# Router logits from unnormalised rows, one Perceiver layer on one NeuronCore

## The reference

```python
x = x + xattn(_layernorm(x), ctx_1024, w1_w, w1_b, w2_w, w2_b)
x = x + attn(_layernorm(x), q_w, q_b, k_w, k_b, v_w, v_b, o_w, o_b)
x = x + ffn(_layernorm(x), gate_w, wg, wu, wd)
```

```python
logits = x_flat @ gate_w.T
top_v, top_i = jax.lax.top_k(logits, K)
probs = jax.nn.softmax(top_v)
...
hidden = jax.nn.silu(x_flat @ wge.T) * (x_flat @ wue.T)
acc + we[:, None] * (hidden @ wde.T)
```

## Time and profile before

| | |
|---|---|
| median of 3 runs | 630.2 us (629.74 to 630.58) |
| profiled execution, time | 631.73 us |
| its span, first to last instruction | 629.8 us |
| PE busy | 605.1 us (96%) |
| PEld busy | 517.9 us (82%) |
| DVE busy | 458.3 us (73%) |
| ACT busy | 336.7 us (53%) |
| POOL busy | 262.6 us (42%) |
| mean granted TensorE clock | 0.985 |
| DMA over the span | 244 GB/s |

### The profile page before, as it was taken

The page is one execution under the profiler, slowest core; times in us unless marked ns, Lnnn a source line. Parts: engine busy times, 40 slices in busy tenths (PEclk is TensorE's granted clock), DMA queues, the critical chain, the costliest instruction groups (busy, mean ns, idle before and its releaser), DMA issues.

```text
span 629.8 us, 10827 instructions
## 1 busy us (share of the span) xinstructions
PE 605.1 (96%) x4033; PEld 517.9 (82%) x4033; DVE 458.3 (73%) x812; ACT 336.7 (53%) x603; POOL 262.6 (42%) x318
## 2 busy tenths in 40 slices
PE   8999999899999999998999898999999999999995
PEld 7889988898889988996667676888888888888884
DVE  4877688767977698768888957876767676776851
ACT  4547523672257423563776671665665657565550
POOL 4317920684157532694544542034241423334222
PEclk9999999999999999999999986999999999999999
DMA  8978887899869746862000355899999999999952
GB/s 286 333 301 232 270 316 202 225 281 289 296 195 290 214 115 175 242 173 67 2 2 2 135 215 210 319 328 347 330 339 348 311 357 320 362 330 347 337 186 83
DMA packets 66131, 152.89 MB, mean 243 GB/s; under 512 B 7632, under 2 KB 47952, under 8 KB 55184
## 3 DMA queue, kind: packets, MB, share of 16 engines
q1 hardware_dynamic: 61712, 146.04, 69.4%
q0 software_dynamic: 4368, 6.16, 4.6%
HBM read 121.91 MB, written 31.59 MB: 244 GB/s over the span
## 4 chain that ended last, share of the span: by engine, by line
PE 72%; DVE 9%; POOL 7%; DMA 4%; ACT 4%; issue 3%; POOLq 0%; DVEq 0%; ACTq 0%; SPq 0%
PE psum L1687 17%; PE psum L1297 13%; PE psum L1422 13%; PE psum L1704 10%; PE psum L1462 9%; POOL wide_low L592 4%; PE psum L1372 2%; DMA region_a<-turned_up 2%; DVE head_max L961 2%; DVE region_a L966 1%; POOL wide_high L590 1%; PE psum L1338 1%; PE psum L1302 1%; ACT wide_high L679 1%; PE psum L1505 1%
## 5 line engine op out<-in xcount | busy, mean ns | idle before, releaser
L679 ACT ACTIVATE wide_high<-region_a 128x1024 fp32r<-128x1024 f32 (+1 forms) x108 | 106.6, 997 | 99.7 <-PE psum L1687 92.6
L1127 DVE TENSOR_TENSOR wide_low<-region_a,wide_high 128x1024 fp32r<-128x1024 f32 x92 | 112.2, 1222 | 63.8 <-ACT wide_high L679 63.8
L592 POOL TENSOR_TENSOR wide_low<-region_a,wide_high 128x512 fp32r<-128x512 f32 x64 | 82.5, 1291 | 18.3 <-ACT wide_high L679 14.3
L1704 PE MATMUL psum<-region_a,region_w 128*128 128x256 f32 x368 | 83.4, 379 | 0.5 <-ACT region_w L679 0.5
L1462 PE MATMUL psum<-turned_high,wide_low 128*128 128x256 f32 x256 | 79.6, 311 | 2.4 <-DVE turned_low L1038 1.5
L1687 PE MATMUL psum<-wide_low,turned_high 128*128 128x512 f32 x184 | 79.2, 431 | 0.1
L1704 PEld LDWEIGHTS psum<-region_a,region_w 128*128 128x128 f32 x368 | 69.6, 190 | 11.0 <-issue 0.9
L1687 PE MATMUL psum<-wide_high,turned_low 128*128 128x512 f32 x184 | 73.0, 397 | 0.0
L1687 PE MATMUL psum<-wide_high,turned_high 128*128 128x512 f32 x184 | 72.7, 395 | 0.0
L1462 PE MATMUL psum<-turned_high,wide_high 128*128 128x256 f32 x256 | 72.4, 283 | 0.0
L1462 PE MATMUL psum<-turned_low,wide_high 128*128 128x256 f32 x256 | 72.2, 282 | 0.0
(11 more groups left out here) (221 smaller groups left out, 1225.3 us busy)
## 6 DMA issues: line engine op xcount, KB each, us to landing
region_a<-turned_up SPq DMA_DIRECT2D x23, 2048.0 KB, 9.7
region_a<-turned_down SPq DMA_DIRECT2D x23, 1024.0 KB, 6.8
region_a<-ctx_dram SPq DMA_DIRECT2D x16, 1024.0 KB, 9.0
turned_up<-region_w SPq DMA_DIRECT2D x64, 256.0 KB, 4.2
region_w<-L_ffn_wg_dram SPq DMA_DIRECT2D x16, 512.0 KB, 6.1
region_w<-L_ffn_wu_dram SPq DMA_DIRECT2D x16, 512.0 KB, 6.0
region_w<-L_ffn_wd_dram SPq DMA_DIRECT2D x16, 512.0 KB, 5.6
turned_down<-region_w SPq DMA_DIRECT2D x32, 256.0 KB, 3.8
```

Source lines behind the costliest of these rows:

```text
L592: nc.gpsimd.tensor_tensor(val_lo[:, g % 4], ctx_sb[n][:, g * PAIR:(g + 1) * PAIR, :], val_hi[:, g % 4].bitcast(F32), ALU.subtract).then_in ...
L679: return nc.scalar.activation(dst, src, ACT.Copy)
L1127: nc.vector.tensor_tensor(w_lo[:, k % RING], group_of(k), w_hi[:, k % RING].bitcast(F32), ALU.subtract).then_inc(low_ready, 1)
L1704: last = nc.tensor.matmul(to[:, 0:D], hidT[n][:, ic * P:(ic + 1) * P], rows, start=ic == 0, stop=ic == IC - 1)
```

## The change

- The logits are taken from the parts of x3. With a gate whose mean over the 256 features is taken away (`gate`), the mean of the row drops out: logits * sd = x2n @ gate * sd2 + heads @ (o_w.T @ gate) + o_b @ gate. Here x2n is the second normalisation's row (its transpose `x2nT` is there already) and sd2 its deviation.
- In the attention stage TensorE does, inside `local_weigh(n)`: the gate's mean by a product with 1/256 (n = 1), `gate_of_output` (n = 5), `gate_of_rows` for two tiles at each of n = 6 to 9, and `gate_of_heads` for tiles 0 to 6 at n = 8 to 14; all go into free columns of bank 6. ScalarE's `local_out` copies three of the results out. GpSimd centres the gate at unit 3 and scales and adds the rows' part at unit 11.
- Behind the last heads one tile's `gate_of_heads` is left, then one addition on VectorE gives `seen`, on which the picks work. `rows_turn3`, `rows_turned3` and `logits` go away.
- VectorE's `output(4)` moves behind the picks, and its `shifted(4)` and the product `behind * rstd` behind the slots' last step but two. Part 3 of `x3n` goes from VectorE to GpSimd, part 4 from VectorE to ScalarE, behind `high(1)` and `high(2)`.
- SP: a second load of `o_w` (256 KB) and one of `o_b` as columns are new; `load_up(1)` goes before the stores and waits for the last value product.
- `WARM_ROUTED` goes from 1, 1, 4, 2, 0, 1 to 2, 2, 7, 4, 2, 1.

```diff
+GATE_MEAN, GATE_CENTRED, GATE_OUT, GATE_SCALED = 1, 3, 5, 11
+GATE_ROWS = {6: (0, 1), 7: (2, 3), 8: (4, 5), 9: (6, 7)}
+GATE_HEADS = {8: [0], 9: [1], 10: [2, 3], 11: [4], 12: [5], 14: [6]}
-WARM_ROUTED = [1, 1, 4, 2, 0, 1]
+WARM_ROUTED = [2, 2, 7, 4, 2, 1]
...
+            sp.wait_ge(pv_done, BATCH * PAIRS + FIRST)
+            sp.dma_start(o_again, o_w.rearrange("(c p) n -> p c n", p=P)).then_inc(output_again, 16)
             sp.wait_ge(local_done, len(WORK))
             load_up(0)
+            sp.wait_ge(localpv_done, len(WORK))
+            load_up(1)
             for s in range(DUOS):
...
-            load_up(1)
             load_down(0)
...
+                if n == GATE_CENTRED:
+                    pool.wait_ge(heads_ready, GATE_MEAN + 1)
+                    nc.gpsimd.tensor_tensor(gate, gwT, gate_mean[:, :].rearrange("p (a e) -> p a e", a=1).broadcast_to([P, DC, E]),
+                                            ALU.subtract).then_inc(gate_step, 1)
...
+                if n == GATE_SCALED:
+                    pool.wait_ge(heads_ready, max(GATE_ROWS) + 1)
...
-            for s in range(2):
+            for s in (0, 1, 3):
...
             root3(2)
-            rows_turned3(0)
             root3(3)
...
+            rows_normed3(2, 1)
+            high(1)
+            high(2)
             root3(4)
-            for s in range(2, len(LAST_ROWS)):
-                rows_turned3(s)
-            high(1)
+            rows_normed3(4, 2)
...
-            output(4)
-            normalise_rows(3)
-            normalise_rows(4)
-
-
-            dve.wait_ge(p3_done, len(LAST_ROWS) + 1)
-            seen = bank[4][:, 0:TILES * E].rearrange("p (t e) -> p t e", t=TILES)
+            shifted(2)
+            inverse_root(3)
+
+
+            dve.wait_ge(rows_gated, 1)
+            dve.wait_ge(gate_done, 1)
+            then(nc.vector.tensor_tensor(seen, heads_logits.rearrange("p (t e) -> p t e", t=TILES), gate_rows, ALU.add))
...
-            nc.vector.tensor_tensor(behind[:, :], top[1][:, :], top[0][:, :], ALU.subtract).then_inc(behind_ready, 1)
+            then(nc.vector.tensor_tensor(behind[:, :], top[1][:, :], top[0][:, :], ALU.subtract))
+            output(4)
...
             then(last)
+            shifted(4)
+            nc.vector.tensor_tensor(behind[:, :], behind[:, :], rstd[:, :], ALU.mult).then_inc(behind_ready, 1)
...
+            def gate_of_rows(t):
+                pe.wait_ge(x2T_ready, t // TPB + 1)
+                for c in range(DC):
+                    nc.tensor.matmul(rows_logits[:, t * E:(t + 1) * E], x2nT[:, c, t * P:(t + 1) * P], gate[:, c, :], start=c == 0, stop=c == DC - 1)
+
+            def gate_of_heads(t):
+                for c in range(DC):
+                    last = nc.tensor.matmul(heads_logits[:, t * E:(t + 1) * E], headsT[:, c, t * P:(t + 1) * P], gate_out[:, c * E:(c + 1) * E],
+                                            start=c == 0, stop=c == DC - 1)
+                return last
...
-            rows_turn3(0)
+            pe.wait_ge(heads_ready, len(WORK))
+            gate_of_heads(TILES - 1).then_inc(gate_done, 1)
             output_rows(4)
-            rows_turn3(1)
-            logits(0)
-            rows_turn3(2)
-            logits(1)
-            rows_turn3(3)
-            rows_turn3(4)
-            for s in range(2, len(LAST_ROWS)):
-                last = logits(s)
-            last.then_inc(p3_done, 1)
```

More of the change, by code:

```diff
@@ L886, in tile_hidT @@
                     copy(hidT[n][:, half * BANK:(half + 1) * BANK], bank[4 + half]).then_inc(hidT_ready, 1)
-            high(2)
             act.wait_ge(behind_ready, 1)
@@ L1530, in local_weigh @@
                     pe.wait_ge(x1_ready, BATCH + FIRST)
+                if n == GATE_MEAN:
+                    for c in range(DC):
+                        nc.tensor.matmul(mean_sum, even_share[:, :], gwT[:, c, :], start=c == 0, stop=c == DC - 1)
+                if n == GATE_OUT:
+                    gate_of_output()
+                for r in GATE_ROWS.get(n, []):
+                    gate_of_rows(r)
+                for r in GATE_HEADS.get(n, []):
+                    gate_of_heads(r)
                 for strip, lo, hi in ([(0, 0, P)] if t == 0 else [(1, 0, WIN), (2, WIN, P)]):
@@ L1564, in output_rows @@
                 last.then_inc(p2c_done, 1)
-            def rows_turn3(s):
-                t0, t1 = LAST_ROWS[s]
-                pe.wait_ge(x3_ready[s], t1 - t0)
-                for c in range(DC):
-                    for t in range(t0, t1):
-                        last = turn(bank[ROWS_BANK[s]][:, (c * (t1 - t0) + t - t0) * P:(c * (t1 - t0) + t - t0 + 1) * P], x3n[:, t, c * P:(c + 1) * P])
-                last.then_inc(p3_done, 1)
             for n in range(len(WORK)):
@@ L1599, in _ @@
             local_weigh(len(WORK) - 1)
-            def logits(s):
-                pe.wait_ge(p3_act, s + 1)
-                for t in range(*LAST_ROWS[s]):
-                    for c in range(DC):
-                        last = nc.tensor.matmul(bank[4][:, t * E:(t + 1) * E], x3nT[:, c, t * P:(t + 1) * P], gwT[:, c, :],
-                                                start=c == 0, stop=c == DC - 1)
-                return last
-            rows_turn3(0)
-            output_rows(4)
-            rows_turn3(1)
-            logits(0)
-            rows_turn3(2)
-            logits(1)
-            rows_turn3(3)
-            rows_turn3(4)
-            for s in range(2, len(LAST_ROWS)):
-                last = logits(s)
-            last.then_inc(p3_done, 1)
+            pe.wait_ge(heads_ready, len(WORK))
+            gate_of_heads(TILES - 1).then_inc(gate_done, 1)
+            output_rows(4)
             def keep_warm(times):
```

73 lines of the change are left out of this document (49 added, 24 removed).

## The result

| | before, same job | changed kernel |
|---|---|---|
| median | 629.97 us (629.36 to 630.58, 4 runs) | 637.09 us (636.37 to 642.14, 4 runs) |
| ratio, 95% interval | | 1.0115 (1.0080 to 1.0151) |
| profiled execution, time; span | 631.73; 629.8 us | 636.37; 634.1 us |
| PE, PEld busy | 605.1, 517.9 us | 607.9, 522.7 us |
| mean granted clock | 0.985 | 0.991 |

The change makes the kernel 7.1 us slower by the medians. The forecast was 629.8 (627.0 to 633.6): wrong, and outside its range. A second comparison (after_again) gave 636.84 us and a ratio of 1.0115 (1.0091 to 1.0140).

What follows compares the result with a forecast made beforehand. The prediction took TensorE to bound the attention stage, then a chain of waits through picks, stores and gathers, then TensorE again. +5.8 - 3.8 - 2.4 = -0.4 us gave 629.8 us, range 627.0 to 633.6.

Steps and rivals of the forecast that it cites:

- Part 1: Attention stage: 38 small products on TensorE delay the end of the last value product (T) by 5.8 us.
- the prediction's count: Attention stage: products at 0.198 us each, less TensorE's pauses they fill, add 5.2 us.
- the replay: Attention stage: replaying the four engine queues with the trace's durations gave 6.1 us for the added products.
- Rival A: Attention stage: weight loads hide behind neighbours' columns, so the small products cost 3.8 us; total 627.8 us, chance 0.20.
- Part 2: Router behind T, the last value product's end: first pick at T + 1.2 instead of 7.7, token list at T + 12.2.
- Part 3: Stores and gathers behind T: gathered rows at T + 17.1 instead of T + 20.9, -3.8 us (bounds -4.5 and -0.6).
- rival D: Row stores wait for the 2 MB load ahead, if it lands after T + 9: 1.6 us, total 631.4, chance 0.05.
- Rival C: Before the token gather: GpSimd waits for a spare gather taking 6.2 us; rows at T + 20.3, total 634.2, chance 0.13.
- Part 4: First expert tile: full TensorE clock and shorter turning save 2.4 us (bounds 0 and -2.4).
- rival B: First expert tile: the clock stays low after sparse TensorE work, saving 0 there; total 632.2 us, chance 0.17.

Runs made afterwards that it cites:

- after_again: The changed kernel unchanged, timed and traced a second time against the kernel before: 636.84 us, ratio 1.0115.
- e1: The kernel before with the 38 eight-column products added at the change's places, their results unread: 636.81 us, ratio 1.0128; stage 86.1 us.
- e2: The changed kernel with `load_up(1)` put back behind the four stores of the normalised rows: 637.70 us, ratio 1.0119.
- e5: The changed kernel with the spare gather taken from `x` and issued before the wait for the stores: 633.27 us, ratio 1.0039.
- e12: The changed kernel with the last store of rows issued by ScalarE on its own queue: 638.56 us, ratio 1.0114.
- e3: The kernel before with more idle products between the router's steps (7, 4, 2 in place of 4, 2, 0): 632.14 us, ratio 1.0019.
- e11: The kernel before with 22 of the 38 eight-column products added, without the 16 of the residual part: 633.98 us, ratio 1.0066.
- e9: The changed kernel with the early spare gather from `x` and the residual's store behind the first tile's down weights: 634.92 us, ratio 1.0081.
- e14: The changed kernel with last store on ScalarE's queue, early spare gather from `x`, and residual's store behind the first down weights: 634.38 us, ratio 1.0054.
- e6: The kernel before with more idle products (7, 4, 2) and the residual's store behind the first tile's down weights: 629.28 us, ratio 0.9980.
- e10: The kernel before with more idle products, residual's store behind the first down weights, and early spare gather from `x`: 628.85 us, ratio 0.9984.
- e4: The changed kernel with the 1 MB residual store issued ahead of the last store of normalised rows: 638.41 us, ratio 1.0108.
- e13: The changed kernel with the last store on ScalarE's queue and the early spare gather from `x`: 636.12 us, ratio 1.0070.

## Why the prediction was wrong

**Part 1, +5.8: right in kind, 0.6 too small.** T moved by the stage's +6.4, and e1 shows that the 38 products alone do it. The term mis-sized is "0.198 us for one": over the stage they make TensorE busy for 0.222 each (in the chain 0.247 in fours, 0.225 in twos). 38 of them are 8.45 us, more than the 7.5 that was to be the upper bound, and the pauses give back 2.0, where the prediction's count had 2.3. Its +5.8 lay between that count's 5.2 and the replay's 6.1, so a part of its nearness is a choice between two values and not a reading. Rival A (they hide, 3.8) is out.

**Part 2: right.** First pick T + 1.5 (1.2 forecast), token list written at T + 12.4 (12.2). At the list 5.0 us of the picks' 6.3 were left.

**Part 3, -3.8: the step that failed is the store's landing.** The store was issued at T + 8.9 (8.4) and "2.6 later" became 4.1: 2.6 belonged to a store with no load ahead of it, as e2's 2.5 shows (share 0.00 from 376 to 380, the store at 379.66), and with the 2 MB load first the engines are full until 384, near T + 13. The spare gather took 3.2 (3.1). Rows: T + 19.1 instead of 17.1, a term of -1.8. This is rival D, which had a chance of 0.05 and a price of 1.6: the load landed at T + 9.9, later than the T + 9 that D asked for, and the price was 1.5. The sum had reckoned that the queue would be clear by T + 9 to 10 and the last store free; in the trace the last of the three early stores lands at T + 10.9, after the last store's issue. Rival C named the right object (GpSimd waits for the spare gather) at the wrong time: it did not take longer, it began later. Without the wait for it the rows come 3.1 us earlier (e5).

The Trainium skill, DMA: Bandwidth & Descriptors, section Queues, rings and completion order, has the descriptors of one queue consumed in ring order. The trace agrees as far as it goes: stores issued behind the load landed in 8.2 us by the middle value, 2.2 before, though the first of them landed 0.8 before the load itself. Whether this order decides here is open: in e12 the store on another queue was no sooner, with full engines (share 1.06) and 1 MB more issued ahead of it.

**Part 4, -2.4: failed, and for two reasons.** The clock was not full at the tile (0.60, 0.83, 0.74 from 384 to 396), after a stretch (380 to 384) in which TensorE's records fill 2.25 of 4 us; that is rival B, whose condition I had written down. In after_again it was 0.65 in 372 to 376, 1.00 from 380 to 388 and 0.50 in 392 to 396, with the same start of the down products behind T. But the larger error is the layout of the chain behind the tile's first products. e3 has the full clock in the kernel before and gains nothing, because ScalarE's next pass needs `up(2)`. I had gone through ScalarE's copies and VectorE's subtractions and stopped at "the next stop is VectorE"; the load behind it, 7.7 to 10.1 us in the earlier trace rows and 9.4 here, was never priced. Rows to down products was +1.0 instead of -2.4; after_again repeats it with 17.3, and the code of the kernel before took 15.8 (e1), 16.5 and 16.7 (e11), so the size of the +1.0 is uncertain and its sign is not.

**Sum.** Errors of 0.6, 2.0 and 3.4 turn -0.4 into +5.6; -0.7 from the stage's start and -0.7 from the rest of the loop make the +4.3 of the two spans, within rounding. The bounds of part 3 (-4.5 and -0.6) held its error, those of part 4 (0 and -2.4) did not, since I had no case in which the loop starts later than before. I gave the cases in which several come together almost nothing, though they may well have a common cause, which no run here isolates: a transfer that is late makes the rows late, which leaves TensorE idle ahead of the tile, where the clock can fall, and lets the next load start late. The rest to the 7.1 of the medians is the spread of single executions.

**What stays open.** Why `up(2)` takes 9.3 us from issue to landing in e9 and 8.7 in e14, and 7.5 in e6 and e10, with only the second tile's down weights ahead of it in all four. What the order of a queue costs a store apart from full engines: e12 with `load_down(0)` held back until the store is issued wasn't run. What the full clock gives in e6: the store moved alone wasn't run either. Which part of the early picks' 5.0 us could be had with the stores out of the way altogether. A version with the small products merged into other products wasn't tried.

## What to carry to other kernels

A product moved out of a waiting stretch into a full one is paid at nearly its full length (here 8.45 us of products for 6.4 us of stage), and what it saves must be followed to the next two stops, transfers included, before it is booked. Here 5 us won on the picks met a store, a spare gather and a weight load one after the other, each of which had been hidden. A wait for something that isn't needed yet (the spare gather) is cheap only as long as another chain is longer; that is the first thing to move when a chain is shortened. A load placed earlier costs the small transfers issued after it (3.8 us to landing instead of 2.3 here), and with full DMA engines another queue was no way out (5.0 in e12).

## What was not expected of the hardware

- A store of 256 KB was followed by the operation that waits for it 2.5 us after issue with idle engines ahead of it (e2), 4.1 behind a 2 MB load, 5.3 with 3 MB issued ahead on another queue (e12), 5.9 behind 3 MB on its own (e4), 6.5 in e13 and e14.
- A gather of 128 rows landed in 2.7 us on quiet engines, 5.2 against 2 MB (e9), 6.3 against 3 MB (e2) and 6.9 against the 2 MB load and the early stores (e5's spare gather).
- Small products (128 stationary columns, 8 moving, float32) took 0.247 us each in fours among other products, and 0.198 behind the transposes after T in the kernel before (four products).
- In the kernel before the larger counts of idle products gave the full clock up to the tile (e3, 0.50 in 376 to 380, then 1.00 from 380 to 396). With the same 7, 4, 2, 1 the changed kernel had 0.60 in 384 to 388, behind a stretch of 2.25 busy of 4 us; its second trace had 1.00 there and 0.50 in 392 to 396. So the same code doesn't get the same clock at the same place each time.
